# A two-layer attention and mixture-of-experts kernel: last-stage biases in the second attention's buffers, reordered loads and memsets, first plan made in the attention's tail

## The reference

```python
x = x + tanh(g_xattn[0]) * attention0(layernorm(x), ctx)        # 8 heads of 64, queries x, keys and values ctx
x = x + tanh(g_ffn[0])   * experts0(layernorm(x))               # top 2 of 8, silu(x W1) * (x W3), W2, width 512
x = x + tanh(g_xattn[1]) * attention1(ctx, layernorm(x), mask)  # 4 heads, keys: masked ctx and the latents
x = x + tanh(g_ffn[1])   * experts1(layernorm(x))               # top 4 of 16, width 256, with biases:
#   h = silu(x @ W1[e].T + b1[e]) * (x @ W3[e].T + b3[e]);  y += (h @ W2[e].T + b2[e]) * w[e]
```

## Time and profile before

| | us |
|---|---|
| median of 3 runs (lowest, highest) | 2112.01 (2111.58, 2114.26) |
| the profiled execution | 2113.48, span 2111.7 |
| PE busy | 1932.3 (92%) |
| POOL, DVE, ACT busy | 1147.6, 1338.0, 930.0 |
| attention0, from the start to its barrier | to 733 |
| experts, layer 0 | 733 to 1071 |
| attention1 | 1071 to 1727 |
| experts1 | 1727 to the end |
| an iteration of attention0, of attention1 | 21, 18.5 |
| biases, three loads of 2048 KB | 15.9 median from issue to landing |

### The profile page before, as it was taken

The page is one execution under the profiler, slowest core; times in us unless marked ns, Lnnn a source line. Parts: engine busy times, 40 slices in busy tenths (PEclk is TensorE's granted clock), DMA queues, the critical chain, the costliest instruction groups (busy, mean ns, idle before and its releaser), DMA issues. The chain is left out here.

```text
span 2111.7 us, 39938 instructions
## 1 busy us (share of the span) xinstructions
PE 1932.3 (92%) x11418; PEld 1348.0 (64%) x11418; DVE 1338.0 (63%) x4050; ACT 930.0 (44%) x2321; POOL 1147.6 (54%) x1375
## 2 busy tenths in 40 slices
PE   5999999999999459999939999999999839999997
PEld 4777777777777348888825555555555525666664
DVE  3677777777777453222336888888888734566564
ACT  2444444434343233233216767666667503333332
POOL 1344444444444345445526888888888723454554
PEclk8999999999999679999979999999999758999999
DMA  6011111111107013333311111111112754555555
GB/s 170 27 31 37 32 35 36 31 39 28 40 27 260 9 26 53 54 52 51 52 32 34 51 51 52 56 56 53 54 54 69 253 167 98 89 92 88 94 89 75
DMA packets 140294, 142.24 MB, mean 67 GB/s; under 512 B 31626, under 2 KB 130674, under 8 KB 139832
## 3 DMA queue, kind: packets, MB, share of 16 engines
q1 hardware_dynamic: 94282, 86.60, 13.9%
q0 software_dynamic: 37888, 44.51, 13.3%
q10 hardware_dynamic: 7918, 8.57, 1.3%
HBM read 89.88 MB, written 51.94 MB: 67 GB/s over the span
## 5 line engine op out<-in xcount | busy, mean ns | idle before, releaser
L779 POOL TENSOR_SCALAR prob<-prob,rc 100x363 f32<-100x363 f32 x256 | 157.0, 623 | 354.6 <-DVE rc L634 354.6
L1826 POOL DMA_INDIRECT out<-y,xr x115 | 178.0, 1548 | 210.2 <-DVE y L1859 138.1
L1932 PE MATMUL psG<-expert_w,xgT 128*128 x460 | 222.0, 606 | 3.0 <-ACT xgT L1893 3.0
L980 PE MATMUL psJ<-wkv,cTn 96*121 96x512 f32 x384 | 177.7, 600 | 0.0
L1843 DVE TENSOR_TENSOR pre<-psG,bias 128x512 f32<-128x512 f32 x115 | 79.5, 691 | 144.6 <-PE psG L1932 104.1
L558 ACT ACTIVATE prob<-psS,nm 100x361 f32<-100x361 f32 x256 | 141.5, 561 | 53.8 <-DVE nm L629 47.6
L1525 POOL DMA_INDIRECT acc<-y,slots x57 | 90.3, 1584 | 136.5 <-DVE y L1619 131.6
L629 DVE TENSOR_REDUCE nm<-psS 100x2 f32<-100x722 f32 x128 | 115.0, 898 | 70.8 <-PE psS L457 70.6
L1432 POOL DMA_INDIRECT rows<-row,pos_of x128 | 137.1, 1071 | 35.6 <-issue 30.1
L1596 DVE TENSOR_TENSOR hid<-psU,gate 128x512 f32<-128x512 f32 x57 | 39.4, 691 | 159.3 <-PE psU L1716 159.3
L1893 ACT ACTIVATE xgT<-psX 128x256 f32<-128x256 f32 x115 | 44.0, 383 | 212.6 <-PE psX L1923 131.9
(11 more groups left out here) (307 smaller groups left out, 5110.1 us busy)
## 6 DMA issues: line engine op xcount, KB each, us to landing
xr<-rows SPq DMA_DIRECT2D x115, 136.5 KB
expert_w<-in_L_ffn_moe_w SPq DMA_DIRECT2D x8, 1024.0 KB
bias<-in_L_ffn_b ACTq DMA_DIRECT2D x3, 2048.0 KB, 15.9
ctx<-in_ctx SPq DMA_DIRECT2D x32, 181.5 KB
cT<-in_ctxT SPq DMA_DIRECT2D x32, 180.5 KB
cT<-in_ctxT SPq DMA_DIRECT2D x64, 90.2 KB
expert_w<-in_L_ffn_moe_w SPq DMA_DIRECT2D x8, 512.0 KB
expert_w<-in_L_ffn_W1T SPq DMA_DIRECT2D x16, 256.0 KB
```

The lines of the kernel that those rows point to most:

```text
L779: g.tensor_scalar(prob[:, q, :], prob[:, q, :], rc[:, q:q + 1], 1.0, ALU.mult, ALU.mult).then_inc(prob_done, 1)
L980: mm = t.matmul(ph[0:rows, 0:cols], lhs, wt[:, k, :], start=k == 0, stop=k == 1)
L1826: g.indirect_dma_start(acc, bass.IndirectOffsetOnAxis(row_token[:, j % RING, :], 0), y[:, j % 4, :], None, compute_op=ALU.add).then_inc(sc ...
L1932: mm = t.matmul(psG[:, r, :], xT[:, r, k, :], w13[:, bass.ds(e, 1), k, :], start=k == 0, stop=k == 1)
```

## The change

- `attention0`: SP loads batch 2 with 0 and 1, ahead of `fill`; `load_attention1` moves into the loop, at b = 2 after the loads of batch 5. The first plan is made at the end of VectorE's and PE's queues, as `attention1` does it. `experts` loses the plan and the waits for it, and VectorE computes the rest of the weights for all eight experts.
- `attention1`: `ctx`, `sq`, `kv` and `prob` become views into one tile `late`, into which the five loads of the biases go (`b2`, then experts 0 to 5 and 6 to 15 of b1 and b3), each after the semaphores that show its part free. Slots of `kv` are numbered (b + 1) % 3. The memset of `kv` covers two of five column blocks and is POOL's; SP's first load of x waits for nothing, and the context waits for the one memset of `ctx`, now VectorE's first instruction. In SP's loop the context goes ahead of x.
- `experts1`: the three loads are gone, the biases are read from `late`.

```diff
@@ attention0, SP
-                for b in range(2):
+                for b in range(3):
                     load_x(b)
 ...
                     load_c(b)
                 fill(s, dram, c)
-                load_attention1(nc, s, a, c)
-                load_x(2)
-                load_c(2)
                 for b in range(B):
 ...
+                    if b == 2:
+                        load_attention1(nc, s, a, c)
@@ attention0, PE, end
+                t.wait_ge(plan, PLANNED - 1)
+                t.matmul(psY[0:1, 2 * P:3 * P], tf[:, 5:6], ident[:, :], start=True, stop=True)
 ...
@@ attention0, VectorE, end
+                then(v.tensor_tensor(f[:, 0, :], c["base"][:, 0:E0], c["region"][:, 0:E0], ALU.subtract))
 ...
+                v.wait_ge(plan, PLANNED)
+                v.tensor_copy(c["tile_s"][:, :], psY[0:1, 2 * P:3 * P])
 ...
@@ attention1, buffers
+        for parts, dims in ((CH, (2, NCH, C)), (CH, (NCH + 2, I1)), (CH, (3, NCH + 2, 2 * I1)), (N, (4, K1))):
+            size = math.prod(dims)
+            names = "abc"[0:len(dims)]
+            views.append(c["late"][0:parts, taken:taken + size].rearrange(
 ...
+            taken += size
+        ctx, sq, kv, prob = views
+        b2, b13 = bias_views(c)
+        def load_bias(engine, lo, hi):
+            engine.dma_start(b13[:, lo:hi, 0, :], a["L1_ffn_b1"][lo:hi].partition_broadcast(P)).then_inc(c["bias_in"], 16)
+            engine.dma_start(b13[:, lo:hi, 1, :], a["L1_ffn_b3"][lo:hi].partition_broadcast(P)).then_inc(c["bias_in"], 16)
@@ attention1, SP
-                s.wait_ge(ready, 1)
                 for i in range(-4, B + 1):
+                    if i == -3:
+                        s.wait_ge(ready, 1)
+                    at(i + 3, load_c)
                     at(i + 4, load_x)
-                    at(i + 3, load_c)
+                    if i == B - 1:
+                        s.wait_ge(ct_mm, 2 * B)
+                        s.wait_ge(ssB, B)
+                        s.wait_ge(o_mm, pairs * (B - 2))
+                        s.dma_start(b2, a["L1_ffn_b2"].partition_broadcast(P)).then_inc(c["bias_in"], 16)
+                    if i == B:
+                        s.wait_ge(o_mm, pairs * B)
+                        load_bias(s, 6, E1)
                     at(i - 1, store)
+                    if i == B - 1:
+                        s.wait_ge(o_mm, pairs * (B - 1))
+                        load_bias(s, 0, 6)
@@ attention1, VectorE, start (ScalarE waits for padded, PE for neither)
-                for e in range(E1):
-                    v.memset(c["base"][:, e:e + 1], float(e * REGION))
-                v.memset(kv[96:CH, :, :, :], 0.0)
-                v.memset(ctx[96:CH, :, NCH - 1, :], 0.0)
+                v.memset(ctx[96:CH, :, NCH - 1, :], 0.0).then_inc(ready, 1)
+                v.wait_ge(ready, 1)
+                v.tensor_scalar(c["token"][:, :], c["token"][:, :], float(-TOKENS), None, ALU.add)
 ...
@@ attention1, POOL, start
-                g.wait_ge(ready, 1)
+                g.memset(kv[96:CH, :, 0:2, :], 0.0).then_inc(padded, 1)
+                g.wait_ge(padded, 1)
@@ experts, layer 0
-                if L0:
-                    for e in range(2):
-                        g.wait_ge(w_high, e + 1)
-                        g.tensor_tensor(w13[:, e].bitcast(F32R), w13[:, e], w_hi[:, e].bitcast(F32), ALU.subtract).then_inc(w_low, 1)
-                g.wait_ge(plan, PLANNED + 1)
 ...
-                    for e in range(2, E):
+                    for e in range(E):
@@ experts1
-                v.wait_ge(bias_in, 16 * 3)
+                v.wait_ge(c["bias_in"], 16 * BIAS_LOADS)
 ...
-                for k in range(3):
-                    s.dma_start(bias[:, :, k, :], a[("L1_ffn_b1", "L1_ffn_b3", "L1_ffn_b2")[k]].partition_broadcast(P)).then_inc(bias_in, 16)
```

More of the change, by code:

```diff
@@ L1 @@
+import math
 from contextlib import ExitStack
@@ L114, in build @@
         experts(nc, maker, a, dram, c, 0)
-        attention1(nc, maker, a, dram, c)
-        experts1(nc, maker, a, dram, c)
+        second = ExitStack()
+        with second:
+            sb, ps, sem = maker(second)
+            c.update(late=sb("late", [P, 3 * E1 * F1]), bias_in=sem("bias_in"))
+            attention1(nc, maker, a, dram, c)
+            experts1(nc, maker, a, dram, c)
 def expert_views(c, layer):
@@ L281, in router_tiles, with bias_views @@
     )
+def bias_views(c):
+    b2 = c["late"][:, 0:E1 * F1].rearrange("p (e f) -> p e f", e=E1)
+    b13 = c["late"][:, E1 * F1:3 * E1 * F1].rearrange("p (e k f) -> p e k f", e=E1, k=2)
+    return b2, b13
+BIAS_LOADS = 5
 def attention0(nc, maker, a, dram, c):
@@ L312, in attention0 @@
         slot_w = r["slot"][:, :, :, 1].bitcast(F32)
+        f, fi = sb("tilef0", [P, 3, E0]), sb("tilei0", [P, 2, E0], I32)
+        ahead, past = sb("tileu0", [P, E0, E0]), sb("tilege0", [P, 2, E0])
+        tf, first = sb("tilet0", [P, 6]), sb("tilefirst0", [P, E0])
+        plan = sem("plan0")
         x_in, c_in = sem("x_in0"), sem("c_in0")
@@ L759, in _, with then @@
                         v.tensor_scalar(c["bo1"][:, :], c["bo1"][:, :], c["tg"][0:N, 1:2], None, ALU.mult)
+                steps = Count(plan)
+                def then(ins):
+                    n = steps.inc(ins)
+                    v.wait_ge(plan, n)
+                then(v.tensor_tensor(f[:, 0, :], c["base"][:, 0:E0], c["region"][:, 0:E0], ALU.subtract))
+                then(v.tensor_copy(fi[:, 0, :], f[:, 0, :]))
+                then(v.tensor_scalar(fi[:, 1, :], fi[:, 0, :], P.bit_length() - 1, None, ALU.arith_shift_right))
+                then(v.tensor_copy(f[:, 1, :], fi[:, 1, :]))
+                then(v.tensor_tensor(ahead[:, :, :], c["upto"][:, 0:E0, 0:E0], f[:, 1, :].unsqueeze(1).to_broadcast([P, E0, E0]), ALU.mult))
+                then(v.tensor_reduce(f[:, 2, :], ahead[:, :, :], AX, ALU.add))
+                then(v.tensor_tensor(past[:, 0, :], c["tile"][:, :].to_broadcast([P, E0]), f[:, 2, :], ALU.is_ge))
+                then(v.tensor_reduce(tf[:, 0:1], past[:, 0, :], AX, ALU.add))
+                then(v.tensor_tensor(past[:, 1, :], past[:, 0, :], f[:, 1, :], ALU.mult))
+                then(v.tensor_reduce(tf[:, 1:2], past[:, 1, :], AX, ALU.add))
+                then(v.tensor_tensor(tf[:, 2:3], c["tile"][:, :], tf[:, 1:2], ALU.subtract))
+                then(v.tensor_scalar(tf[:, 2:3], tf[:, 2:3], float(P), None, ALU.mult))
+                then(v.scalar_tensor_tensor(tf[:, 3:4], tf[:, 0:1], float(REGION), tf[:, 2:3], ALU.mult, ALU.add))
+                then(v.tensor_scalar(tf[:, 2:3], tf[:, 0:1], float(E0 - 1), None, ALU.min))
+                then(v.tensor_tensor(first[:, :], c["tile"][:, :].to_broadcast([P, E0]), f[:, 2, :], ALU.is_equal))
+                then(v.tensor_reduce(tf[:, 4:5], first[:, :], AX, ALU.max))
+                then(v.scalar_tensor_tensor(tf[:, 5:6], tf[:, 4:5], 16.0, c["landed"][:, :], ALU.mult, ALU.add))
+                v.wait_ge(plan, PLANNED)
+                v.tensor_copy(c["tile_s"][:, :], psY[0:1, 2 * P:3 * P])
+                v.tensor_copy(c["tile_e"][:, :], psY[0:1, 0:P])
+                v.tensor_copy(c["tile_r"][:, :], psY[0:1, P:2 * P])
             @block.gpsimd
@@ L1328, in _ @@
                 v.memset(gmax[:, :], -1.0)
-                v.tensor_scalar(c["token"][:, :], c["token"][:, :], float(-TOKENS), None, ALU.add).then_inc(ready, 1)
-                v.wait_ge(ready, 1)
+                for e in range(E1):
+                    v.memset(c["base"][:, e:e + 1], float(e * REGION))
                 for i in range(-4, B + 2):
@@ L1635, in _ @@
             def _(s):
-                s.wait_ge(plan, PLANNED + 1)
                 def load(j):
```

48 lines of the change are left out of this document (18 added, 30 removed).

## The result

The changed kernel takes 2079.69 us (median of 4 runs, 2076.21 to 2080.36) against 2111.8 (4 runs, 2109.17 to 2114.26): ratio 0.9845, 95% interval 0.9828 to 0.9862, some 33 us faster. The forecast was 2070.6, a gain of 41.4. The profiled execution took 2079.23 with a span of 2077.5, so the two traces differ by 34.2 us of span.

The account below looks back on a forecast made before the run. TensorE, busy 92% of the span, was taken as the bound except at the start and three stage changes; gains 11.5 + 7.8 + 10.9 + 11.2 = 41.4 us gave 2070.6 us, range 2063 to 2085.

Parts of the forecast that it names:

- A, stall: Kernel start: with batch 2's loads moved ahead, ScalarE's wait for the context and TensorE's stall go; 5.5 us.
- A, clock: Kernel start: the 13 us at half clock after the stall run at full clock; 6.0 us saved.
- A, to the first barrier: Whole gain of the kernel's start, stall plus clock; 11.5 us, between 5.5 and 12.
- B, to TensorE's start: First experts stage: plan fits VectorE's idle time before the barrier, so TensorE starts earlier; 7.8 us.
- B, whole first experts stage: The same 7.8 us gain from the earlier plan, counted over the whole first experts stage.
- C, start: Second attention's start: x goes out at once, context after one memset; 10.9 us, ends 8.5 and 11.8.
- C, order in the loop: Second attention's loop: context ahead of x costs 0; x has 0.9 us or more in hand, costs from a 4.6 us landing.
- D: Last stage: biases loaded in the second attention's tail, removing waits and some half clock; 11.2 us, between 6.4 and 13.
- near end: First experts stage: each VectorE correction beside a ScalarE cast takes 2.22 us, against 4.39 at the far end.
- Rival 2: Second attention's tail: bias loads delay stores or scatters and the barrier; 2 to 8 us, 2072.6 to 2078.6, chance 0.08.
- third rival: Second attention's loop: x lands late behind the context, delaying VectorE; at 0.5 us an iteration 2084.6; chance 0.06.
- sign of being wrong: Second attention's loop: VectorE waits for x, or iterations take longer than the 18.5 us of now.

Follow-up runs that it names:

- before_again: The kernel before, unchanged, traced again on one chip with other runs; 2110.37 us.
- after_again: The changed kernel, unchanged, traced again on the same chip as other runs; ratio 0.9843 to the kernel before.
- order_only: The kernel before with one edit: in the second attention's loop, from iteration 0 on, context is issued ahead of x; ratio 1.0043, 9.1 us slower.
- before_masks3: The kernel before with only a third buffer for the mask bytes instead of two; ratio 0.9927, 15.4 us gained.
- masks3_c_first: The changed kernel, its own order (context ahead of x), with a third buffer for the mask bytes; ratio 0.9736, median 2058.36 us.
- x_later: The changed kernel, but in the second attention's loop SP issues x only once the context's three loads have landed; ratio 0.9828.
- x_first: The changed kernel with x issued ahead of context again in the second attention's loop, from iteration 0 on; ratio 0.9824, median 2076.24 us.

## Why the prediction was right, and where it was not

The time, 2079.7, is inside the range of 2063 to 2085 and 9.1 above the forecast; it is just outside the forecast's own 2063 to 2077. Luck has a part in it: the range was built from the low ends of four gains, and the 9 us that the loop's order took stand in none of them; it held because it was wide. Step by step, in us; "first two traces" are before and after, "14 traces" the mean of the seven kernels without a part less that of the seven with it, over the same marks:

| step | forecast | first two traces | 14 traces | alone, timed |
|---|---|---|---|---|
| A, stall | 5.5 | 5.5 | | |
| A, clock | 6.0 | 4.7, then -0.7 in the stage's tail | | |
| A, to the first barrier | 11.5 | 9.4 | 8.7 | 9.9 (7.0 to 12.7) |
| B, to TensorE's start | 7.8 | 7.9 | 7.9 | |
| B, whole first experts stage | 7.8 | 7.6 | 7.4 | 6.1 (3.0 to 9.3) |
| C, start | 10.9 | 11.3, of which 9.4 left at batch 0's router product | 10.2 there | 10.6 (7.8 to 13.3) |
| C, order in the loop | 0 | -8.6 | -9.1 | -9.1 (-11.8 to -6.1) |
| loop, batches 27 to 31 | 0 | +3.0 | scatter | |
| D | 11.2 | 13.4 | 12.9 | 11.8 (7.6 to 15.8) |

9.4 + 7.6 + 9.4 - 8.6 + 3.0 + 13.4 = 34.2, the difference of the spans. One pair of traces can mislead: batches 27 to 31 took 68.2 before and 65.2 after, but 66.3 in before_again and 67.2 in after_again, and 65.2 to 68.3 over all 14. The clock's half stretches fall at other times there from trace to trace, so the +3.0 is no gain of the change. By the 14 traces the sum is 8.7 + 7.4 + 10.2 - 9.1 + 12.9 = 30.1, inside what the ratio's interval allows (29.1 to 36.3).

**A.** The stall went whole. The clock's share was mis-sized: half of 12.44 busy us is 6.2, but TensorE, faster now, meets a wait of 0.96 for GpSimd, and 10.15 are kept in all at batch 3's copy. 0.7 goes again at the end of the stage, where the last batch's products run at half clock (0.50 in the changed kernel over the 10 us in which the kernel before had 0.65). The trace of before was also one of the slow ones: after the same stall its clock was at half until 53.7, in order_only and before_masks3 only until about 45, and batch 3's copy stood at 60.65 to 64.19 in the seven kernels with the stall against 53.12 to 53.68 in the seven without. Less the stall's 5.5, these marks put the clock's share at 1.7 to 5.2 us, an estimate; the forecast's 6.0 was above all of it.

**B and C's start** came out to within half a microsecond at the marks that were forecast, the corrections at the near end taken (2.21 each beside the casts). No 4 us step shows, and no gather held the corrections up. Behind the marks some is lost again: 0.5 in the rest of the first experts stage, 1 to 2 while the second attention's pipeline fills.

**D** gained 3.6 for the landing of x (3.2 forecast), 6.6 up to the first hidden tile (1.9 + 4.5 forecast) and 3.2 behind it, where 1.6 was taken of a possible 2.9. The clock behind the first hidden tile is now full. Of the 3.2, 2.3 lie between the first and the second hidden tile (5.90 before, 3.62 after); the six other kernels without part D took 4.80 to 6.00 there, the six others with it 3.56 to 3.67, so the gain of the clock is 1.1 to 2.4 and the forecast's 1.6 was a fair middle. Rival 2 did not come: the tail is as long as before.

**C in the loop** is the step that failed: "It costs from a landing of 4.6 us on". The question put was whether x comes in time, by its cover of 0.9 us. The trace of before held the answer to another one: in the earlier trace rows VectorE waits 1.40 for the context, so it was already the context that ended last, with no cover at all, and an edit that puts another load right behind it was costed at nothing. The third rival had the place and, at 0.5 an iteration, about the price (0.3 came), and the chance of 0.06 was too low. The prediction's own sign of being wrong, iterations longer than the 18.5 of now, used a number that was too high: the kernel before takes 18.16, the changed one 18.48 and 18.65. It was also the wrong mechanism: the third buffer, which touches no x, removes the cost entirely (masks3_c_first against after_again, iterations 17.72 and 18.65), and VectorE waits for the context in every kernel without that buffer, for x in neither of the two. Why a context followed by x is usable 0.2 us later at the median is open: x_later kept most of the delay (3.77) with neither x nor the store beside the loads, x_first (3.71) has the store right behind them.

The loop that closes through the load, in one iteration of the kernel before (timeline, 1205 to 1236):

```profile
1209.72 1.01 POOL L1403 TENSOR_SCALAR mb<-m 100x361 f32<-100x361 uint8 x1
1210.79 0.31 SPq L912 DMA_DIRECT2D ctx<-in_ctx  x1
1211.15 0.35 SPq L913 DMA_DIRECT2D ctx<-in_ctx  x1
1211.56 0.31 SPq L914 DMA_DIRECT2D m<-in_mask  x1
...
1214.31 0.88 DVE L1182 BATCH_NORM_STATS2 cst<-ctx 121x6 f32<-121x192 f32 x3 [0.87 <-DMA m<-in_mask]
```

GpSimd's mask ends at 1210.73 and SP issues 0.06 later. From the end of the last issue, the mask of 100 x 361 bytes, to the use are 2.44 us; one semaphore counts the mask and the two pieces of the context, so which of the three landed last is not shown. The Trainium skill ("DMA: Bandwidth & Descriptors", Anatomy of one DMA — SWDGE (gpsimd) path) gives a DMA from GpSimd a fixed part of about 2.0 us that doesn't grow with its size; this one is SP's, and the trace is of that order. No run here tries a smaller load. The Trainium skill's rule to issue a DMA early and wait for it late (same page, Rules for kernel authors) is what the third buffer does: 15.4 us on the kernel before.

## What to carry to other kernels

A small wait that stands in every iteration on a transfer (here 0.87 us) can be a loop closed through a DMA, as it was here: before reordering anything beside it, ask what lets the transfer start, and give that a buffer more. Cost an edit in a loop by the load that already ends last, not only by the one that is moved. Read a gain of a few microseconds from more than one pair of traces: the +3.0 here was scatter. The kernels whose loop hangs on the landing seem to scatter more (five runs of one spread over 3.7 to 7.3 us, with the third buffer over 1.4 to 3.6), but so few runs do not show it firmly.

## What the runs showed of the hardware that was not expected

The same three loads, issued in the same way, were usable after 3.4 to 5.2 us. In order_only, 1.15 us in which TensorE stood waiting in an otherwise full loop was followed by some 10 us at half clock; in the changed kernel 1.41 us (at 1283) was not, the clock of that stretch is 1.00 and stays so through 1298:

```profile
1278.00:1282.00 4.00, 3.73 (x17) 2.01 (x16) 2.07 (x9) 2.82 (x6) 3.52 (x7) 1.00 0.52 155
1282.00:1286.00 4.00, 2.60 (x12) 1.43 (x12) 3.44 (x16) 0.96 (x4) 2.00 (x4) 1.00 0.02 8
```

Four gathers on GpSimd took 1.87 to 2.11 us beside VectorE's corrections, against 0.98 later in the stage, and the corrections were not slowed: 2.21 each. The kernel before shows the same, 1.81 to 1.90 beside its six corrections. The gathers start 2.17 to 2.42 apart, close to a correction's 2.21. The Trainium skill's rule that the prediction weighed ("SBUF — State Buffer", Who interferes with whom) has VectorE and GpSimd exclude each other in such a pair. The trace agrees in so far as GpSimd is the slower one here and TensorE's start did not move; that this lock is the cause is not shown.
